# The output stage of a two-layer graph network: leaky slope as one VectorE maximum, and two of three loads issued by ScalarE

## What is computed

```python
h = h @ W_lin + b_lin
h_in = h
feat = (h @ W_gat).reshape(N, 8, 32)
...
e = exp(e - m[dst])
s = segment_sum(e, dst)
out = segment_sum(feat[src] * (e / s[dst])[:, :, None], dst)
out = out.reshape(N, 256) + gat_bias
out = leaky_relu(out, 0.01)
return h_in + out              # and the caller: x = x + that
```

## Time and profile before

| what | value |
| --- | --- |
| median of 3 runs | 6000.13 us (5995.2 to 6009.43) |
| the profiled execution: its own time | 6002.02 us |
| its span, first to last instruction | 6000.1 us |
| mean granted TensorE clock | 0.904 |
| busy share: TensorE, VectorE, GpSimd, ScalarE | 90%, 82%, 63%, 53% |
| output stage: first load issued, last output added | 5774.95 us, 5993.16 us |

### The profile page before, as it was taken

The page is one execution under the profiler, slowest core; times in us unless marked ns, Lnnn a source line. Parts: engine busy times, 40 slices in busy tenths (PEclk is TensorE's granted clock), DMA queues, the critical chain, the costliest instruction groups (busy, mean ns, idle before and its releaser), DMA issues. The chain is left out here.

```text
span 6000.1 us, 128155 instructions
## 1 busy us (share of the span) xinstructions
PE 5427.5 (90%) x26094; PEld 4291.0 (72%) x26094; DVE 4908.2 (82%) x12464; ACT 3153.2 (53%) x10275; POOL 3755.0 (63%) x4022
## 2 busy tenths in 40 slices
PE   8978888888888888888999998988999999999988
PEld 5556666666666666667999996766777777777766
DVE  4469999999999999996777775777787787878864
ACT  3446666566666665643333334555555565555533
POOL 1147666766666666644444446777777777777733
PEclk9999999999999999999999997787777777777789
DMA  5679889998988888872222224777777777777767
GB/s 176 211 223 291 284 284 290 290 289 281 289 281 285 285 282 285 283 232 83 83 85 85 84 85 141 218 218 219 219 217 218 216 221 218 221 218 217 220 201 229
DMA packets 723032, 1313.66 MB, mean 219 GB/s; under 512 B 109087, under 2 KB 502131, under 8 KB 722420
## 3 DMA queue, kind: packets, MB, share of 16 engines
q0 software_dynamic: 200192, 634.41, 37.3%
q1 hardware_dynamic: 444802, 422.18, 23.6%
q10 hardware_dynamic: 77426, 250.73, 10.9%
HBM read 964.16 MB, written 342.73 MB: 218 GB/s over the span
## 5 line engine op out<-in xcount | busy, mean ns | idle before, releaser
L826 PE MATMUL bank<-ev,oh 128*128 128x264 f32 x7040 | 2275.3, 453 | 94.5 <-DVE ev L1294 93.5
L534 POOL DMA_INDIRECT Gf<-kv_tab,srcs x1564 | 1573.4, 1006 | 721.3 <-issue 511.2
L534 POOL DMA_INDIRECT Gf<-ft_tab,srcs x1564 | 1603.5, 1025 | 484.1 <-issue 412.8
L826 PEld LDWEIGHTS bank<-ev,oh 128*128 128x128 f32 x7040 | 1459.8, 220 | 348.3 <-DVE ev L1294 128.6
L826 PE MATMUL bank<-Gf 128*128 128x128 f32 (+3 forms) x6480 | 1263.6, 346 | 21.8 <-ACT Gf L815 15.4
L1294 DVE TENSOR_TENSOR ev<-Gf,ex 128x528 f32<-128x528 f32 x1760 | 1228.5, 698 | 2.0 <-ACT ex L698 1.2
L826 PE MATMUL bank<-qs,oht 128*128 128x256 f32 x3520 | 955.1, 394 | 227.1 <-DVE prod L1203 226.9
L826 PEld LDWEIGHTS bank<-Gf 128*128 128x128 f32 x6480 | 966.2, 191 | 221.5 <-issue 98.6
L630 ACT ACTIVATE absd<-lane,dlocs 128x128 f32<-128x128 f32 x3520 | 1113.0, 389 | 3.6 <-DVE bms L1176 3.6
L826 PEld LDWEIGHTS bank<-qs,oht 128*128 128x128 f32 x3520 | 598.9, 190 | 438.6 <-issue 372.1
L1309 DVE SCALAR_TENSOR_TENSOR acc<-acc,same,bank 128x264 f32<-128x264 f32 x1540 | 732.0, 475 | 22.7 <-PE bank L826 20.8
(11 more groups left out here) (160 smaller groups left out, 6086.7 us busy)
## 6 DMA issues: line engine op xcount, KB each, us to landing
sums<-acc ACTq DMA_DIRECT2D x440, 528.0 KB
qs<-q_tab SPq DMA_DIRECT2D x880, 128.0 KB
qs<-dst_tab SPq DMA_DIRECT2D x880, 128.0 KB
Gf<-sums SPq DMA_DIRECT2D x196, 132.0 KB, 2.1
kv_tab<-Gf SPq DMA_DIRECT2D x98, 260.0 KB, 2.1
Gf<-in_x SPq DMA_DIRECT2D x196, 128.0 KB, 2.1
Gf<-kv_tab,srcs POOLq DMA_INDIRECT x1564
Gf<-ft_tab,srcs POOLq DMA_INDIRECT x1564
```

The lines of the kernel that those rows point to most:

```text
L534: pool.indirect_dma_start(out=rows[layer][:, m % SLOTS[layer], k, :], out_offset=None, in_=tab, in_offset=bass.IndirectOffsetOnAxis(ap=src ...
L826: return nc.tensor.matmul(o, a, r, start=first, stop=end)
```

## The change

In the output stage the leaky slope is now one VectorE instruction, max(0.01 b, b), in place of two ScalarE activations, a matrix `neg` and the fourth product of TensorE. It is a new semaphore, `f_lr`, that GpSimd and the output addition wait for. ScalarE, which has no activation left in the stage, issues the loads of `fin_xm` and `fin_h`, six tiles ahead of the store that it issues in the same pass; their addresses are constants now. SyncE issues the load of `fin_in` alone and waits for VectorE's last reading of the buffer (`f_att`) in place of TensorE's.

```diff
@@ SyncE
             def f_load(t):
                 k = t % FR
-                wait(sp, S_["f_lin"], t - FR + 1)
+                wait(sp, S_["f_att"], t - FR + 1)
                 e = sp.value_load(endstep[0:1, bass.ds(t, 1)], min_val=0, max_val=NS * P - 4 * P + 3)
                 sp.dma_start(fin_in[k], sums[bass.ds(e, P, step=4), :]).then_inc(S_[f"f_in{k}"], 16)
-                sp.dma_start(fin_xm[k], xm_tab[bass.ds(t * P, P), :]).then_inc(S_[f"f_in{k}"], 16)
-                sp.dma_start(fin_h[k], h2t_tab[bass.ds(t * P, P), :]).then_inc(S_[f"f_in{k}"], 16)
@@ GpSimd
                 pool.wait_ge(S_["f_att"], t + 1)
-                wait(pool, S_["f_neg"], t - 2)
+                wait(pool, S_["f_lr"], t - 2)
@@ ScalarE
-            act.activation(neg, ident[:, :], ACT.Copy, scale=-1.0).then_inc(S_["f_neg0"], 1)
-            for t in range(NT + 3):
+            for t in range(NT + FR):
                 if t < NT:
-                    act.wait_ge(S_["f_bias"], t + 1)
-                    wait(act, S_["f_out"], t - 2)
-                    wait(act, S_["f_lin"], t - 2)
-                    act.activation(fin_p[t % 3], fin_b[t % 3], ACT.Relu).then_inc(S_["f_pos"], 1)
-                    act.activation(fin_n[t % 3], fin_b[t % 3], ACT.Relu, scale=-0.01).then_inc(S_["f_neg"], 1)
-                if t >= 3:
-                    u = t - 3
-                    rows = min(P, N - u * P)
-                    act.wait_ge(S_["f_out"], u + 1)
-                    act.dma_start(out[u * P:u * P + rows, :], fin_o[u % 3][0:rows, :]).then_inc(S_[f"f_st{u % 3}"], 16)
+                    k = t % FR
+                    wait(act, S_["f_lin"], t - FR + 1)
+                    act.dma_start(fin_xm[k], xm_tab[t * P:(t + 1) * P, :]).then_inc(S_[f"f_in{k}"], 16)
+                    act.dma_start(fin_h[k], h2t_tab[t * P:(t + 1) * P, :]).then_inc(S_[f"f_in{k}"], 16)
+                u = t - FR
+                if u < 0:
+                    continue
+                rows = min(P, N - u * P)
+                act.wait_ge(S_["f_out"], u + 1)
+                act.dma_start(out[u * P:u * P + rows, :], fin_o[u % 3][0:rows, :]).then_inc(S_[f"f_st{u % 3}"], 16)
@@ TensorE
-            pe.wait_ge(S_["f_neg0"], 1)
...
-                mm(o, ident[:, :], fin_xm[k], False, False)
-                pe.wait_ge(S_["f_neg"], t + 1)
-                mm(o, neg, fin_n[t % 3], False, True).then_inc(S_["f_lin"], 1)
+                mm(o, ident[:, :], fin_xm[k], False, True).then_inc(S_["f_lin"], 1)
@@ VectorE
                     dve.wait_ge(S_["f_lin"], u + 1)
+                    dve.wait_ge(S_["f_lr"], u + 1)
...
                 if t < NT:
                     dve.wait_ge(S_["f_max"], t + 1)
                     V.reciprocal(d[:, H:2 * H], d[:, 0:H]).then_inc(S_["f_rec"], 1)
+                if 2 <= t <= NT + 1:
+                    u = t - 2
+                    dve.wait_ge(S_["f_bias"], u + 1)
+                    V.scalar_tensor_tensor(fin_p[u % 3], fin_b[u % 3], 0.01, fin_b[u % 3],
+                                           ALU.mult, ALU.max).then_inc(S_["f_lr"], 1)
+                if t < NT:
```

More of the change, by code:

```diff
@@ L264, in build @@
         v_gb = steps[:, 2 * D:3 * D]
-        neg = carve(P)
         fin_h = [carve(D) for _ in range(FR)]
         fin_in, fin_xm = [[carve(w) for _ in range(FR)] for w in (HV, D)]
-        fin_a, fin_b, fin_p, fin_n, fin_o, fin_d = [[carve(w) for _ in range(3)] for w in (D, D, D, D, D, 2 * H)]
+        fin_a, fin_b, fin_p, fin_o, fin_d = [[carve(w) for _ in range(3)] for w in (D, D, D, D, 2 * H)]
         ohs = [v[:, k * SPAN:(k + 1) * SPAN] for v in (oht[:, :, :, :].rearrange("p a k n -> p (a k n)"),
@@ L288, in build @@
             m_tr0 m_tr1 m_tr2 m_cp0 m_cp1 m_cp2 m_mm0 m_mm1 m_mm2 m_w1 m_gelu f_tr f_cp f_mm f_w
-            m_sxm m_sh2 m_sft m_rdacc m_fo m_xmb f_neg0 f_lin m_xb m_hb m_h1b f_in0 f_in1 f_in2 f_in3 f_in4 f_in5 f_max f_rec f_att f_bias f_pos f_neg f_out f_st0 f_st1 f_st2""".split():
+            m_sxm m_sh2 m_sft m_rdacc m_fo m_xmb f_lin m_xb m_hb m_h1b f_in0 f_in1 f_in2 f_in3 f_in4 f_in5 f_max f_rec f_att f_bias f_lr f_out f_st0 f_st1 f_st2""".split():
             S_[name] = sem(name)
```

## The result

The changed kernel takes 5939.64 us (median of 4, 5933.81 to 5944.22), where the kernel before took 6001.45 us beside it: a ratio of 0.9902, with an interval of 0.989 to 0.9914. So 61.8 us are gained, 34 were forecast. On the base of the median that the prediction started from, 6000.13 us, the ratio makes 5941 us (5934 to 5949 by its interval), so that the range's 5942 can't be told from it.

The account below looks back on a forecast made before the run. SyncE's issuing bounds the old stage, the DMA engines the new: start 5771.3 + 1.4, plus 182.3 us of DMA work at share 0.95, plus 10.9 for the end, gives 5966 us; forecast 5953 to 5978, whole range 5942 to 5988.

Parts of the forecast that it names:

- SyncE's issuing is the bound: Output stage before the change: SyncE needs 2.05 us to issue a tile's three loads; without two issues, 1.1.
- Nothing is gained: Rival: the DMA engines already bound the output stage; 5988 to 6012 us, chance 0.10.
- The slope costs nothing and gains nothing by itself: Output stage: two activations leave unmissed, a quarter of TensorE's products goes, VectorE's added 0.42 us is covered by waiting.
- DMA work of 1.79 us a tile at a share of 0.95, taken as the bound: Output stage after the change: DMA engines bound it, 173.2 us of work taking 182.3 us.
- ScalarE, 1.2 to 1.45 us a tile: Output stage: ScalarE's three issues at 0.34 to 0.43 us each plus 0.05 between two, below the DMA engines' 1.79.
- TensorE, 1.30 us a tile: Output stage: a quarter of the products goes, taking TensorE from 1.73 to 1.30 us a tile.
- VectorE, 1.3 to 1.5: Output stage: VectorE's turn grows from 1.07 us to 1.3 to 1.5 with one added instruction priced at 0.42.
- The early start: Start of the output stage: ScalarE issues six pairs of loads at 5771.3 us, data moving some 1.4 us later.
- the first: Rival: a full second queue makes load packets cheaper, 1.53 us a tile, end 5939; under 5953 us, chance 0.13.
- the store's way round: Rival: VectorE's addition waits for a store three turns back, queued behind two loads; slower, up to 6019 us, chance 0.03.
- TensorE's clock: Rival: gaps let TensorE fall to 1.2 GHz, 2.6 us a tile; slower, up to 6041 us, chance 0.02.

Follow-up runs that it names:

- loads_only: Kernel before, with the loads of xm and h issued by ScalarE four tiles ahead, keeping the two activations and fourth product: 5964.16 us, ratio 0.9945.
- leaky_only: Changed kernel with the loads of xm and h back on SyncE: 6006.29 us, ratio 1.002.
- probe: Changed kernel with eighty 128 KB loads appended: one at a time, SyncE back to back, SyncE and ScalarE together; 300, 288, 326 and 317 GB/s per unit share.
- half_rows: Changed kernel with the same issues, but loads of xm and h bring only 128 of 256 columns: 5936.01 us, ratio 0.9904.
- no_gpsimd: Changed kernel with one xm/h table, six output buffers, only h loaded, and no GpSimd bias addition: 7309.19 us on another chip, ratio 0.9868.
- one_table: Changed kernel with xm and h side by side in one table, one load of 2 KB rows: 5935.85 us, ratio 0.9899.

## Why the prediction was right in direction and short in size

- **SyncE's issuing is the bound**: right. `loads_only`, which moves issues and leaves all the arithmetic, gives 33 us; `leaky_only`, which takes TensorE's and ScalarE's work away and leaves the issues, gives nothing. SyncE dropped out with two of them gone, as said. So *Nothing is gained* did not come true; the prediction calls it its last rival, it is the third in its list.
- **The slope costs nothing and gains nothing by itself**: right as said, but its worth on top of the move was not in the sum as a step. It takes TensorE's 1.73 us and the late store out of the way, 1.85 to 1.57 us a turn. The sum saw it only as "not the bound", because a larger term, 1.79, stood above it.
- **DMA work of 1.79 us a tile at a share of 0.95, taken as the bound**: this is the step that failed. The account gave 1.88 us a tile, and the turns took 1.57. By the queues' rows the engines were busy (75.8 + 26.5)% of 110 us for 70 tiles, 1.61 us a tile, at a share of 1.03. Both factors were wrong: the recorded work fell by a tenth (`probe` shows the effect by itself), and the share is no fraction with a ceiling of 1. The row that said so was on the table: 327 GB/s in ten us. 516 KB at 327 GB/s is 1.62 us. I took the time per packet at partial load for work. `half_rows` then shows that the DMA engines weren't the bound of the changed kernel at all: what took their place is ScalarE's issuing, the next point.
- **ScalarE, 1.2 to 1.45 us a tile**: the value taken was wrong, and outside its upper end. The 0.34 us was the price of an issue after a pause; three in a row cost 0.44 to 0.51 with constant addresses, 1.52 a tile, the bound of the changed kernel. The 0.43 from SyncE's row was nearer, and it belonged to the position in the row of issues, not to the register: `probe` has it with constant addresses.
- **TensorE, 1.30 us a tile**: right, 1.29 in `no_gpsimd`.
- **VectorE, 1.3 to 1.5**: the range held (1.42 without other waits), the reason did not: the instruction itself costs 0.37, and 0.28 is blocking by GpSimd. The prediction said nothing of that. That its price of 0.42 came near the mean of 0.43 in the changed kernel is luck, since that mean is a mix of 0.37 and up to 0.65.
- **The early start** (data from 5772.7 us on): wrong. ScalarE's loads did go out first, but turn 0 waits for the `sums` load, which no one issues earlier.
- **Rivals**: the time fell on the first (packets that get cheaper, 0.13), and that it did so within 1 us is luck. Packets did get cheaper, but to 1.61 us a tile where that rival had 1.53, and its 1.53 / 0.95 = 1.61 happens to lie near the 1.57 that ScalarE's issuing set. The waits of the store's way round exist (`loads_only`, `one_table`), not as a loss. TensorE's clock stayed full.

## What to carry to other kernels

When work moves off the engine that paces a stage, price the new queue by issues in a row, not by one that follows a pause, and then ask of every engine what a turn would be without the waits: here four of them lay between 1.29 and 1.57 us, and each repair uncovered the next within about 0.1 us. DMA busy share at partial load is not work; take the highest GB/s that the trace shows anywhere as what the engines can do at least (327 before, and up to 362 in later runs). Before an instruction is added to VectorE beside GpSimd, look which of the two starts first, for the small ones too.

## What the hardware showed that I had not expected

- A `tensor_scalar` on 128x8 took 0.69 us in place of 0.16 when GpSimd's addition had started before it, which cost 0.4 us a turn and 33 us in all. Nothing was changed but the order of two instructions.
- DMA issues from one engine: 0.33 to 0.34 us after a pause, 0.43 to 0.51 back to back, on SyncE and on ScalarE alike.
- 362 GB/s with 1 KB and 2 KB rows on two queues, with a share of 1.04.
